# A tuned two-layer transformer kernel: the second bf16 part of q and k written by GpSimd's own subtraction instead of by a ScalarE copy

## The chip, the core and the metric

The kernel runs on one core of a Trainium2 chip. The metric is device time in microseconds, of which smaller is better. In the rows below PE is TensorE, DVE is VectorE, ACT is ScalarE, POOL is GpSimd and SP is SyncE, which here only issues DMAs.

## What is computed

The input x has 16 sequences ("batches" below) of 512 tokens and 128 features. Four blocks follow one another, each added to its own input: attention, a gated feed-forward network, a second attention with RMS-normed q and k, and a linear layer with a routed LoRA term.

```
x = x + _L0_attn_ref(_layernorm(x, axis=-1), ...)
x = x + _L0_ffn_ref(_layernorm(x, axis=-1), ...)
x = x + _L1_attn_ref(_layernorm(x, axis=-1), ...)
x = x + _L1_ffn_ref(_layernorm(x, axis=-1), ...)
```

Each attention has 16 heads of 8 features over 512 keys: `scores = softmax(q k^T * scale)`, then `scores @ v`, then a projection. The first attention is called layer 0 below, the second one layer 1.

## The kernel before

**Slots and units.** The 32 attentions (16 batches, two layers) run one after the other, each in a *slot* of 64 *units*. In a unit PE makes one tile of scores for the current attention (`attend_score`, L1203) and one tile of scores for the next one (`max_score`, L1193, 26 units ahead). ACT takes the exponential of the first (L719), and DVE takes the row maxima of the second (L932). Every fourth unit PE multiplies four tiles of exponentials with v (L1218). All other work is put between units by tables (`PE_AT`, `ACT_AT`, `DVE_AT`, `POOL_AT`, `SP_AT`), which give the unit at which an engine's in-order program comes to it. The tables fix the order on each engine, and semaphores fix the rest. From slot 2 to slot 27 layer 0 runs in even slots and layer 1 in odd ones.

**Three bf16 parts.** The score matmuls are bf16, so q and k (f32, tiles `qf` and `kf`, 128x512) are split into three bf16 parts in `qp` and `kp`: part 0 is q rounded, part 1 the rounded residual, part 2 the rounded residual of that. ACT writes `qf` (L748) and part 0 (`take_part0`, L697). POOL forms the residual in place (`residual1`, L585). ACT copies it to bf16 (`take_part1`, L697), and POOL subtracts again (`residual2`, L591).

**From parts to stacks.** When part 2 is there, SP writes the parts to DRAM with three DMAs (`parts_out`, L432: first q's, then k's). When they have landed it reads them back as stacked rows, in two halves of four DMAs each (`stack_half`, L446: `q_stack`, `k_stack`). The first `max_score` of the next attention, at unit 38 of the slot, needs the first half.

**What is near.** In an even slot (the group "M2" of the tables, for layer 1) the order on POOL is: residual of q1, a normalisation of `o_raw` (L597), part 2 of q1, residual of k1, part 2 of k1, then the residuals of the next batch's q0 and k0 (group "P0"), part 2 of k0, `norm_factors` for the third layer norm (L578 and L580), and part 2 of q0. On SP the third quarter of the row maxima (`max_rows`, L453) stands between `parts_out` of k1 and `stack_half`. On ACT `apply_norm` (L725) waits for `norm_factors`, and PE's transposes (L1156) wait for it.

Of the kernel before, what the change touches and what calls it, by code (L numbers as in the profile page):

```python
# [8 lines left out]
ALU = mybir.AluOpType  # L9
# [42 lines left out]
         "M2": {"qt": 16, "kt": 19, "v1": 19},  # L52
         "E": {"pr1": 22, "xt3": 40, "rt": 45, "ct": 65, "out": 68}}
ACT_AT = {"A": {"save0": 36, "save1": 67},
          "P0": {"part0_q0": 8, "part0_k0": 16, "part1_q0": 27, "part1_k0": 27},
          "P0_fast": {"part0_q0": 4, "part0_k0": 8, "part1_q0": 10, "part1_k0": 17},
          "S0": {"xn0a": 44, "xn0b": 58},
          "M1": {"xn1": 25, "xn2": 50, "sq0": 55, "sq1": 58},
          "M2": {"part0_q1": 17, "part0_k1": 21, "part1_q1": 19, "part1_k1": 22},
          "E": {"xn3a": 33, "xn3b": 38, "gexp": 50}}  # L60
DVE_AT = {"A": {"inv0": 43, "inv1": 73},
          "S0": {"st0a": 27, "st0b": 27, "mo0": 31, "fa0": 34},
# [45 lines left out]
def due_table(tables):  # L108

    due = {}  # L110
    for group, b, slot, shift in GROUPS:
        for table in tables:
            for name, at in table[group].items() if group in table else ():
                due.setdefault(name, {})[UNITS * slot + shift + at] = b
    return due


PE_DUE, ACT_DUE, DVE_DUE, POOL_DUE, SP_DUE = (due_table([t]) for t in (PE_AT, ACT_AT, DVE_AT, POOL_AT, SP_AT))
# [5 lines left out]
def at(due, name, t):  # L124

    return due[name][t] if name in due and t in due[name] else None
# [71 lines left out]
def build(nc, T, out_dram):  # L198
    ctx = ExitStack()
    with ctx:  # L200
# [48 lines left out]
        qf = [[sb(f"{c}f{l}", [128, SEQ]) for c in "qk"] for l in (0, 1)]  # L249
        qp = [[sb(f"{c}p{l}", [128, PARTS, SEQ], BF16) for c in "qk"] for l in (0, 1)]  # L250
# [80 lines left out]
        resid1 = [sem(f"{c}_resid1") for c in ("q0", "k0", "q1", "k1")]  # L331
        part0 = [sem(f"part0_{l}") for l in (0, 1)]

        part1 = [sem(f"{c}_part1") for c in ("q0", "k0", "q1", "k1")]
# [219 lines left out]
        def _(pool):  # L554
# [27 lines left out]
            def residual1(l, n, b):  # L582

                pool.wait_ge(part0[l], 2 * b + n + 1)
                pool.tensor_tensor(qf[l][n][:, :], qf[l][n][:, :], qp[l][n][:, 0, :], ALU.subtract  # L585
                                   ).then_inc(resid1[2 * l + n], 1)

            def residual2(l, n, b):

                pool.wait_ge(part1[2 * l + n], b + 1)  # L590
                pool.tensor_tensor(qp[l][n][:, 2, :], qf[l][n][:, :], qp[l][n][:, 1, :], ALU.subtract  # L591
                                   ).then_inc(part2[2 * l + n], 1)

# [56 lines left out]
            for t in TIMES:  # L650
                for n in (0, 1, 2):
                    b = at(POOL_DUE, f"nr{n}", t)
                    if b is not None:
                        newton_round(n, b)
                for n in (0, 1):
                    b = at(POOL_DUE, f"sc{n}", t)
# [5 lines left out]
                b = at(POOL_DUE, "nf1", t)  # L662
                if b is not None:
                    norm_factors(1, b)
                for c in range(NH):
                    b = at(POOL_DUE, f"um{c}", t)
                    if b is not None:
                        up_mul(c, b)
                for l in (1, 0):
                    for n in (0, 1):  # L670
                        b = at(POOL_DUE, f"r1_{'qk'[n]}{l}", t)
                        if b is not None:
                            residual1(l, n, b)
                        b = at(POOL_DUE, f"r2_{'qk'[n]}{l}", t)
                        if b is not None:
                            residual2(l, n, b)
                b = at(POOL_DUE, "nf3", t)
                if b is not None:
                    norm_factors(3, b)
                b = at(POOL_DUE, "mix", t)  # L680
                if b is not None:
                    mix(b)
                b = at(POOL_DUE, "nf0", t)
                if b is not None:
                    norm_factors(0, b)
                b = at(POOL_DUE, "nf2", t)
# [8 lines left out]
        def _(act):  # L695
            def copy(dst, src):
                return act.activation(dst, src, ACT.Copy)  # L697
# [54 lines left out]
                need(act, rows_out[l][n], 48 * b)  # L752
                copy(qp[l][n][:, 0, :], qf[l][n][:, :]).then_inc(part0[l], 1)

            def take_part1(l, n, b):
                act.wait_ge(resid1[2 * l + n], b + 1)
                copy(qp[l][n][:, 1, :], qf[l][n][:, :]).then_inc(part1[2 * l + n], 1)

            def take_max(l, quarter, b):
                act.wait_ge(written[f"m{l}"], 4 * b + quarter + 1)  # L760
                if quarter < 2:
# [39 lines left out]
            for n in (0, 1):  # L801
                if n == 0:
                    act.wait_ge(bq_ready, 1)
                take_qk(0, n, 0)
                take_part0(0, n, 0)
                take_part1(0, n, 0)
            weights_out()
            apply_norm(0, x_in, range(TT), 1)
            for t in TIMES:
# [11 lines left out]
                b = at(PE_DUE, "xt0", t)  # L821
                if b is not None:
                    take("xt0", xnt[0][:, :], b)
                for l in (0, 1):
                    for n in (0, 1):
                        b = at(PE_DUE, (("q0", "k0"), ("qt", "kt"))[l][n], t)
                        if b is not None:
                            take_qk(l, n, b)
                        b = at(ACT_DUE, f"part0_{'qk'[n]}{l}", t)
                        if b is not None:  # L830
                            take_part0(l, n, b)
                        b = at(ACT_DUE, f"part1_{'qk'[n]}{l}", t)
                        if b is not None:
                            take_part1(l, n, b)
                b = at(ACT_DUE, "xn3a", t)
                if b is not None:
                    apply_norm(3, x3, (0, 1), b)
                b = at(ACT_DUE, "xn3b", t)
                if b is not None:
                    apply_norm(3, x3, (2, 3), b)  # L840
                b = at(PE_DUE, "xt3", t)
                if b is not None:
                    take("xt3", xnt[3][:, :], b)
                b = at(ACT_DUE, "gexp", t)
                if b is not None:
                    gate_exp(b)
                b = at(PE_DUE, "ct", t)
                if b is not None:
                    take_coef(b)
                b = at(ACT_DUE, "xn0a", t)  # L850
                if b is not None:
                    apply_norm(0, x_in, (0, 1), b)
                b = at(ACT_DUE, "xn0b", t)
                if b is not None:
                    apply_norm(0, x_in, (2, 3), b)
                b = at(ACT_DUE, "xn1", t)
                if b is not None:
                    apply_norm(1, x1, range(TT), b)
                b = at(PE_DUE, "xt1", t)
                if b is not None:  # L860
                    take("xt1", xnt[1][:, :], b)
                for c in range(NH):
                    b = at(PE_DUE, f"g{c}", t)
                    if b is not None:
                        gate_tanh(c, b)
                    b = at(PE_DUE, f"u{c}", t)
                    if b is not None:
                        take_up(c, b)
                b = at(ACT_DUE, "xn2", t)
                if b is not None:  # L870
                    apply_norm(2, x2, range(TT), b)
                b = at(PE_DUE, "xt2", t)
                if b is not None:
                    take("xt2", xnt[2][:, :], b)
                for half in (0, 1):
                    b = at(ACT_DUE, f"sq{half}", t)
# [488 lines left out]
```

## Time and profile before

| | |
|---|---|
| median of 3 runs | 1851.92 us (1851.39 to 1855.57) |
| the profiled execution | 1849.55 us, of which the span is 1847.7 us |
| busy: PE, DVE | 1711.7 us (93%), 1560.2 us (84%) |
| busy: ACT, POOL | 1419.9 us (77%), 515.4 us (28%) |
| mean granted TensorE clock | 0.978 of full speed |

The busy times say how full an engine is over the whole span. Matmuls are pipelined, so that a busy PE is not PE at its peak. What limits a stretch is read from the chain of work that ended last and from what each idle time waited for. An even slot lasts some 48 us and an odd one some 61 us.

### The profile page before, as it was taken

The numbers are of one execution on the slowest core, as the hardware profiler recorded it, in microseconds if no ns is written. First come the engines' busy times: TensorE is split into PE (matmuls) and PEld (weight loads), VectorE is DVE, ScalarE is ACT, GpSimd is POOL, SyncE is SP. The second block draws the span as 40 slices with busy tenths as digits, with TensorE's granted clock in tenths as the row PEclk, the third lists the DMA queues.
The fourth block names the chain that finished last, engine by engine and source line by source line (L and its number), as shares of the span: only waits on it lengthen the run. The fifth ranks groups of instructions, "written<-read, shape, count | busy, mean of one in ns | idle before, by whom it ended". The sixth has DMA issues, their size and how long they took to land.

```text
span 1847.7 us, 32248 instructions
## 1 busy us (share of the span) xinstructions
PE 1711.7 (93%) x10958; PEld 654.7 (35%) x10958; DVE 1560.2 (84%) x3443; ACT 1419.9 (77%) x2921; POOL 515.4 (28%) x771
## 2 busy tenths in 40 slices
PE   4999899999999999999999999999999999999994
PEld 1233233434333343333334333343433334334333
DVE  3988789898998989898898898989899898888981
ACT  2788678787877978778787877878787787777872
POOL 3124132241222324122141313214122332422311
PEclk9999899999999999999999999999999999999996
DMA  5232324232142422315133151423315242132310
GB/s 126 65 82 73 96 49 127 49 85 80 43 134 48 116 61 65 100 38 139 47 85 90 38 128 37 128 48 81 84 43 133 48 111 59 36 66 77 85 35 24
DMA packets 162646, 141.35 MB, mean 76 GB/s; under 512 B 38762, under 2 KB 144051, under 8 KB 162483
## 3 DMA queue, kind: packets, MB, share of 16 engines
q1 hardware_dynamic: 160562, 138.18, 29.0%
q8 instruction: 88, 1.44, 0.4%
q10 hardware_dynamic: 1920, 1.11, 0.2%
q14 instruction: 76, 0.61, 0.1%
HBM read 77.38 MB, written 55.57 MB: 72 GB/s over the span
## 4 chain that ended last, share of the span: by engine, by line
PE 62%; DVE 12%; ACT 11%; DMA 6%; issue 4%; SPq 3%; POOL 2%; DVEq 0%; POOLq 0%; ACTq 0%
PE ps L1218 19%; PE ps L1203 15%; DVE neg_max L932 8%; PE ps L1193 7%; PE ps L1239 7%; ACT probs L719 6%; PE ps L1156 4%; DMA k_stack<-k_rows 3%; PE ps L1244 3%; PE ps L1232 3%; PE ps L1283 3%; ACT xn L725 2%; PE ps L1289 2%; DMA k_rows<-kp 2%; DVE bn L908 1%
## 5 line engine op out<-in xcount | busy, mean ns | idle before, releaser
L932 DVE TENSOR_REDUCE neg_max<-ps 128x1 f32<-128x512 f32 x2048 | 1305.9, 679 | 131.4 <-PE ps L1193 125.4
L719 ACT ACTIVATE probs<-ps 128x512 f32<-128x512 f32 x2048 | 1099.2, 594 | 272.9 <-PE ps L1203 271.2
L1193 PE MATMUL ps<-k_stack,q_stack 48*128 48x512 bf16 x2048 | 691.0, 391 | 57.9 <-DVE neg_max L932 38.0
L1203 PE MATMUL ps<-q_stack,k_stack 50*128 50x512 bf16 x2048 | 657.5, 387 | 24.1 <-ACT probs L719 14.3
L1218 PE MATMUL ps<-probs,v_aug 128*32 128x512 f32 x4096 | 555.3, 615 | 0.1
L1203 PEld LDWEIGHTS ps<-q_stack,k_stack 50*128 50x128 bf16 x2048 | 153.7, 94 | 593.3 <-ACT probs L719 355.4
L1193 PEld LDWEIGHTS ps<-k_stack,q_stack 48*128 48x128 bf16 x2048 | 162.1, 93 | 215.8 <-DVE neg_max L932 166.3
L578 POOL TENSOR_TENSOR rstd<-vpe,half_neg 128x4 f32<-128x4 f32 x64 | 64.6, 1010 | 268.6 <-DVE vpe L923 268.6
L597 POOL TENSOR_TENSOR o_raw<-o_raw,rden_all 128x512 f32<-128x512 f32 x64 | 81.6, 1276 | 177.9 <-DMA rden_all<-rden_rows 177.9
L1218 PEld LDWEIGHTS ps<-probs,v_aug 128*32 128x32 f32 x4096 | 80.9, 108 | 138.7 <-issue 76.8
L725 ACT ACTIVATE xn<-x,shift,rstd 128x128 f32<-128x128 f32 x192 | 80.7, 487 | 29.2 <-POOL shift L580 29.2
L635 POOL TENSOR_TENSOR coef<-gating,rm 128x64 f32<-128x64 bf16 x64 | 16.8, 294 | 284.4 <-DVE gating L1040 284.4
L585 POOL TENSOR_TENSOR qf<-qf,qp 128x512 f32<-128x512 f32 x32 | 37.2, 1161 | 205.2 <-ACT qp L697 205.2
L628 POOL TENSOR_TENSOR ht<-up,gs 128x512 f32<-128x512 f32 x48 | 61.2, 1276 | 98.2 <-ACT up L697 98.0
L607 POOL TENSOR_TENSOR nw_t<-nw_y 128x128 f32<-128x128 f32 x48 | 19.2, 401 | 214.9 <-DVE nw_y L1012 212.4
L1244 PE MATMUL ps<-wo,o_raw 128*128 128x128 f32 x512 | 67.3, 286 | 9.6 <-POOL o_raw L597 9.6
L1244 PEld LDWEIGHTS ps<-wo,o_raw 128*128 128x128 f32 x512 | 61.2, 196 | 26.6 <-issue 16.0
L1156 PE MATMUL ps<-ident,xn 128*128 128x128 f32 x256 | 46.4, 310 | 23.4 <-ACT xn L725 22.6
L970 DVE TENSOR_TENSOR x<-ps,x 128x512 f32<-128x512 f32 x32 | 22.1, 691 | 42.0 <-PE ps L1283 21.7
L970 DVE TENSOR_TENSOR x<-ps,res 128x512 f32<-128x512 f32 x32 | 21.9, 686 | 39.7 <-PE ps L1244 39.7
L1239 PE MATMUL ps<-xnt,w_up 128*128 128x256 f32 x192 | 54.2, 404 | 0.0
L1239 PE MATMUL ps<-xnt,w_gate 128*128 128x256 f32 x192 | 50.6, 386 | 1.3 <-DVE gs L982 0.6
(104 smaller groups left out, 1520.8 us busy)
## 6 DMA issues: line engine op xcount, KB each, us to landing
q_stack<-q_rows SPq DMA_DIRECT2D x128, 192.0 KB, 3.7
k_stack<-k_rows SPq DMA_DIRECT2D x128, 192.0 KB, 4.8
rden_all<-rden_rows SPq DMA_DIRECT2D x64, 256.0 KB
q_rows<-qp SPq DMA_DIRECT2D x32, 384.0 KB, 2.6
k_rows<-kp SPq DMA_DIRECT2D x32, 384.0 KB, 2.8
q_rows<-qp SPq DMA_DIRECT2D x32, 256.0 KB, 2.9
k_rows<-kp SPq DMA_DIRECT2D x32, 256.0 KB, 2.9
x_in<-in_L_attn_x SPq DMA_DIRECT2D x16, 256.0 KB, 3.3
```

The costliest lines, as they stand in the source:

```text
L578: pool.tensor_tensor(rstd[k][:, :], vpe[k][:, :], half_neg[:, :], ALU.pow).then_inc(rstd_ready[k], 1)
L597: pool.tensor_tensor(o_of(l, b)[:, c, :], o_of(l, b)[:, c, :], rden_all[:, c, :], ALU.mult).then_inc(att_ready[l], 1)
L628: pool.tensor_tensor(ht[:, c, :], up[:, :], gs[:, :], ALU.mult).then_inc(ht_done, 1)
L719: act.activation(probs[:, g % RING, :], home("score", (l, b, u)), ACT.Exp).then_inc(exps, 1)
L725: last = act.activation(xn[k][:, t, :], x[:, t, :], ACT.Identity, bias=shift[k][:, t:t + 1], scale=rstd[k][:, t:t + 1])
L932: dve.tensor_reduce(neg_max[l][:, pair // 2, col:col + 1], home("max", (l, b, n)), AX.X, ALU.max, negate=True).then_inc(max_taken, 1)
L1156: return pe.transpose(dst, src, ident[0:n, 0:n])
L1193: pe.matmul(home("max", (l, b, m)), q_stack[l][row:row + KROWS, pair, tok:tok + 128], k_stack[l][row:row + KROWS, pair, :], start=True, st ...
L1203: pe.matmul(home("score", (l, b, u)), k_stack[l][row:row + AROWS, pair, tok:tok + 128], q_stack[l][row:row + AROWS, pair, :], start=True, ...
L1218: last = pe.matmul(acc[32 * j:32 * j + 32, :], v_of(l, b)[:, kt, 8 * e + 2 * group + pp, :], probs[:, (g + j) % RING, :], start=(s == 0 an ...
L1239: return pe.matmul(dst[:, 256 * half:256 * half + 256], w, xt[:, 256 * half:256 * half + 256], start=True, stop=True)
L1244: last = pe.matmul(by_tile(dst)[:, t, :], o_of(l, b)[:, c, 128 * t:128 * t + 128], wo[l][:, c, :], start=c == 0, stop=c == 1)
```

## The change

ACT's copy `take_part1` goes, with its places in the table. POOL's `residual1` gets a second subtraction of the same operands ahead of the one that it had: it writes part 1 in bf16 straight away. The f32 residual is still formed, for part 2. `residual2` now waits for two semaphores, both of POOL itself. Its lines move by three and more (L591 becomes L594, L697 becomes L700, L719 becomes L722).

```diff
-          "P0": {"part0_q0": 8, "part0_k0": 16, "part1_q0": 27, "part1_k0": 27},
-          "P0_fast": {"part0_q0": 4, "part0_k0": 8, "part1_q0": 10, "part1_k0": 17},
+          "P0": {"part0_q0": 8, "part0_k0": 16},
+          "P0_fast": {"part0_q0": 4, "part0_k0": 8},
...
             def residual1(l, n, b):
 
                 pool.wait_ge(part0[l], 2 * b + n + 1)
+                pool.tensor_tensor(qp[l][n][:, 1, :], qf[l][n][:, :], qp[l][n][:, 0, :], ALU.subtract
+                                   ).then_inc(part1[2 * l + n], 1)
                 pool.tensor_tensor(qf[l][n][:, :], qf[l][n][:, :], qp[l][n][:, 0, :], ALU.subtract
                                    ).then_inc(resid1[2 * l + n], 1)
 
             def residual2(l, n, b):
 
                 pool.wait_ge(part1[2 * l + n], b + 1)
+                pool.wait_ge(resid1[2 * l + n], b + 1)
                 pool.tensor_tensor(qp[l][n][:, 2, :], qf[l][n][:, :], qp[l][n][:, 1, :], ALU.subtract
                                    ).then_inc(part2[2 * l + n], 1)
...
-            def take_part1(l, n, b):
-                act.wait_ge(resid1[2 * l + n], b + 1)
-                copy(qp[l][n][:, 1, :], qf[l][n][:, :]).then_inc(part1[2 * l + n], 1)
```

On POOL, in the middle of slot 2 (the first slot that has the order of all later even ones), stood before (a digit behind a name is the layer):

```order
L585 TENSOR_TENSOR qf1<-qf1,qp1 128x512 [waits part0_1]
L597 TENSOR_TENSOR o_raw01<-o_raw01,rden_all 128x512 [waits rden_in0]
L591 TENSOR_TENSOR qp1<-qf1,qp1 128x512 [waits q1_part1]
L585 TENSOR_TENSOR kf1<-kf1,kp1 128x512 [waits part0_1]
L591 TENSOR_TENSOR kp1<-kf1,kp1 128x512 [waits k1_part1]
L585 TENSOR_TENSOR qf0<-qf0,qp0 128x512 [waits part0_0]
L585 TENSOR_TENSOR kf0<-kf0,kp0 128x512 [waits part0_0]
L591 TENSOR_TENSOR kp0<-kf0,kp0 128x512 [waits k0_part1]
L591 TENSOR_TENSOR qp0<-qf0,qp0 128x512 [waits q0_part1]
```

And in the same place on POOL now:

```order
L585 TENSOR_TENSOR qp1<-qf1,qp1 128x512 [waits part0_1]
L587 TENSOR_TENSOR qf1<-qf1,qp1 128x512
L600 TENSOR_TENSOR o_raw01<-o_raw01,rden_all 128x512 [waits rden_in0]
L594 TENSOR_TENSOR qp1<-qf1,qp1 128x512 [waits q1_resid1,q1_part1]
L585 TENSOR_TENSOR kp1<-kf1,kp1 128x512 [waits part0_1]
L587 TENSOR_TENSOR kf1<-kf1,kp1 128x512
L594 TENSOR_TENSOR kp1<-kf1,kp1 128x512 [waits k1_resid1,k1_part1]
L585 TENSOR_TENSOR qp0<-qf0,qp0 128x512 [waits part0_0]
L587 TENSOR_TENSOR qf0<-qf0,qp0 128x512
L585 TENSOR_TENSOR kp0<-kf0,kp0 128x512 [waits part0_0]
L587 TENSOR_TENSOR kf0<-kf0,kp0 128x512
L594 TENSOR_TENSOR kp0<-kf0,kp0 128x512 [waits k0_resid1,k0_part1]
```

Two more instructions stand in front of part 2 of k1 (the first L594 that writes kp1), and four in front of part 2 of k0; no wait for ACT's copy is left between a residual and part 2. From slot 4 on `norm_factors` stands behind part 2 of k0.

On ACT in the same slot stood before:

```order
L748 ACTIVATE qf1<-ps,qn_scaled 128x512 [waits qt_written]
L719 ACTIVATE probs<-ps 128x512 [waits scores]
L697 ACTIVATE qp1<-qf1 128x512 [waits qrows_out1,qt_read]
L719 ACTIVATE probs<-ps 128x512 [waits pv,scores]
L697 ACTIVATE kp0<-kf0 128x512 [waits krows_out0,k0_read]
L719 ACTIVATE probs<-ps 128x512 [waits scores]
L697 ACTIVATE qp1<-qf1 128x512 [waits q1_resid1]
L748 ACTIVATE kf1<-ps,norm_w 128x512 [waits kt_written]
L719 ACTIVATE probs<-ps 128x512 [waits scores] x2
L697 ACTIVATE kp1<-kf1 128x512 [waits krows_out1,kt_read]
L719 ACTIVATE probs<-ps 128x512 [waits pv,scores]
L697 ACTIVATE kp1<-kf1 128x512 [waits k1_resid1]
```

And now:

```order
L751 ACTIVATE qf1<-ps,qn_scaled 128x512 [waits qt_written]
L722 ACTIVATE probs<-ps 128x512 [waits scores]
L700 ACTIVATE qp1<-qf1 128x512 [waits qrows_out1,qt_read]
L722 ACTIVATE probs<-ps 128x512 [waits pv,scores]
L700 ACTIVATE kp0<-kf0 128x512 [waits krows_out0,k0_read]
L722 ACTIVATE probs<-ps 128x512 [waits scores]
L751 ACTIVATE kf1<-ps,norm_w 128x512 [waits kt_written]
L722 ACTIVATE probs<-ps 128x512 [waits scores] x2
L700 ACTIVATE kp1<-kf1 128x512 [waits krows_out1,kt_read]
```

The two copies that waited for POOL's residual (q1_resid1 and k1_resid1) are gone. The orders of PE, DVE and SP are unchanged.

## Rows read from the trace of the kernel before

**Rows 1.** The page: the chain that ended last, shares by engine

```profile
PE 62%; DVE 12%; ACT 11%; DMA 6%; issue 4%; SPq 3%; POOL 2%; DVEq 0%; POOLq 0%; ACTq 0%
```

**Rows 2.** Groups by form: busy us, mean ns | idle before, releaser

```profile
L697 ACT ACTIVATE kp<-kf 128x512 bf16<-128x512 f32 x64 | 41.0, 641 | 12.9 <-POOL kf L585 12.9
...
L585 POOL TENSOR_TENSOR kf<-kf,kp 128x512 f32<-128x512 f32 x32 | 37.2, 1162 | 12.5 <-ACT kp L697 12.4
...
L591 POOL TENSOR_TENSOR kp<-kf,kp 128x512 bf16<-128x512 f32 x32 | 37.1, 1159 | 41.9 <-ACT kp L697 41.9
```

**Rows 3.** The chain in slot 10, in order of time: start us, us, what

```profile
616.58 0.52 ACT qp L697
...
619.24 1.17 POOL kf L585
...
620.44 0.64 ACT kp L697
...
621.14 1.17 POOL kp L591
...
623.24 2.56 DMA k_rows<-kp
...
627.19 5.49 DMA k_stack<-k_rows
```

**Rows 4.** The chain again, in slots 2 and 24

```profile
180.59 1.16 POOL kp L591
...
1389.38 1.17 POOL kp L591
```

**Rows 5.** Timeline of POOL in slot 10: start us, us, instruction [idle before <-releaser]

```profile
615.16 1.17 POOL L585 TENSOR_TENSOR qf<-qf,qp 128x512 f32<-128x512 f32 x1 [11.43 <-ACT qp L697]
616.28 1.28 POOL L597 TENSOR_TENSOR o_raw<-o_raw,rden_all 128x512 f32<-128x512 f32 x1
617.52 1.17 POOL L591 TENSOR_TENSOR qp<-qf,qp 128x512 bf16<-128x512 f32 x1
619.24 1.16 POOL L585 TENSOR_TENSOR kf<-kf,kp 128x512 f32<-128x512 f32 x1 [0.56 <-ACT kp L697]
621.14 1.16 POOL L591 TENSOR_TENSOR kp<-kf,kp 128x512 bf16<-128x512 f32 x1 [0.74 <-ACT kp L697]
622.26 1.16 POOL L585 TENSOR_TENSOR qf<-qf,qp 128x512 f32<-128x512 f32 x1
623.38 1.17 POOL L585 TENSOR_TENSOR kf<-kf,kp 128x512 f32<-128x512 f32 x1
626.04 1.15 POOL L591 TENSOR_TENSOR kp<-kf,kp 128x512 bf16<-128x512 f32 x1 [1.50 <-ACT kp L697]
627.37 1.01 POOL L578 TENSOR_TENSOR rstd<-vpe,half_neg 128x4 f32<-128x4 f32 x1 [0.17 <-DVE vpe L923]
628.46 0.20 POOL L580 TENSOR_TENSOR shift<-neg_mean,rstd 128x4 f32<-128x4 f32 x1
```

**Rows 6.** Timeline of SP's queue in slot 10

```profile
622.39 1.32 SPq L432 DMA_DIRECT2D k_rows<-kp  x3
624.00 1.30 SPq L453 DMA_DIRECT2D q_stack<-m_parts  x2
625.85 0.81 SPq L446 DMA_DIRECT2D q_stack<-q_rows  x2
```

**Rows 7.** Who waited for whom: us in total, times, longest us

```profile
PE ps L1193 <- DMA k_stack<-k_rows: 14.7, 13, 4.5
```

**Rows 8.** Timeline of PE, in slots 6 and 22

```profile
416.38 0.63 PE L1156 MATMUL ps<-ident,xn 128*128 128x128 f32 x4 [0.44 <-ACT xn L725]
...
1292.71 0.39 PE L1193 MATMUL ps<-k_stack,q_stack 48*128 48x512 bf16 x2 [1.86 <-DMA k_stack<-k_rows]
```

**Rows 9.** Timeline of ACT in slot 10

```profile
629.67 0.87 ACT L725 ACTIVATE xn<-x,shift,rstd 128x128 f32<-128x128 f32 x2
```

**Rows 10.** Timeline of DVE in slot 10

```profile
619.84 0.59 DVE L938 CAST neg_high<-neg_max 128x16 bf16<-128x16 f32 x1
```

More of the change, by code:

```diff
@@ L54 @@
 ACT_AT = {"A": {"save0": 36, "save1": 67},
-          "P0": {"part0_q0": 8, "part0_k0": 16, "part1_q0": 27, "part1_k0": 27},
-          "P0_fast": {"part0_q0": 4, "part0_k0": 8, "part1_q0": 10, "part1_k0": 17},
+          "P0": {"part0_q0": 8, "part0_k0": 16},
+          "P0_fast": {"part0_q0": 4, "part0_k0": 8},
           "S0": {"xn0a": 44, "xn0b": 58},
           "M1": {"xn1": 25, "xn2": 50, "sq0": 55, "sq1": 58},
-          "M2": {"part0_q1": 17, "part0_k1": 21, "part1_q1": 19, "part1_k1": 22},
+          "M2": {"part0_q1": 17, "part0_k1": 21},
           "E": {"xn3a": 33, "xn3b": 38, "gexp": 50}}
@@ L805, in _ @@
                 take_part0(0, n, 0)
-                take_part1(0, n, 0)
             weights_out()
@@ L831, in _ @@
                             take_part0(l, n, b)
-                        b = at(ACT_DUE, f"part1_{'qk'[n]}{l}", t)
-                        if b is not None:
-                            take_part1(l, n, b)
                 b = at(ACT_DUE, "xn3a", t)
```

## Prediction

> **What bounds the kernel now.** I first read the shares of the chain that ended last. PE has 62% of it, DVE 12%, ACT 11%, DMA 6% and POOL 2% [rows 1]. So this is a pipeline of units led by PE, and ACT, which the change relieves, is only a ninth of the chain. POOL, which the change loads, is idle most of the time, but it is on the chain all the same, and the question is where.
>
> The chain in order of time tells. In slot 10 it leaves the pipeline of units at ACT's copies, and goes through POOL's residual of k (619.24), ACT's copy of it to bf16 (620.44), POOL's part 2 of k (621.14), the DMA of the parts to DRAM (from 623.24, 2.56 us) and the DMA that reads the stack back (from 627.19, 5.49 us, so landed at 632.68) [rows 3]. PE's first `max_score` of layer 1 stood waiting for that. The chain takes this route in seven even slots, 2, 10, 12, 14, 18, 22 and 24; the first and the last of them are in [rows 4]. In the others PE mostly waits there too, but something else is as late. In all PE waited 14.7 us in 13 places for a stack [rows 7], up to 1.86 us in one slot [rows 8]; the longest wait, of 4.5 us, is the program's start. So the latency from "part 0 of q1 is there" to "the stack has landed" is what an even slot hangs on, and the change rebuilds its first links.
>
> **ACT: what is removed.** ACT loses 64 copies (16 batches, two layers, q and k). One takes 641 ns [rows 2], and keeps the next instruction off for 0.52 us (at 616.58 in [rows 3]), so 64 x 0.52 = 33 us in all. ACT also loses the waits for POOL's residual ahead of them, 12.9 us before the k copies [rows 2]. Of this only what lies on the chain can shorten anything. In an even slot that is the copy of q1 at 616.58. It delays kf1, thereby part 0 of k1, thereby POOL's residual of k1. But as shown next, POOL will not be free for that residual when it comes earlier. The other copies lie behind the start of the POOL work on which the stack hangs, or beside PE and DVE work. Nothing that they free lets PE pass unit 38 before the stack is there. I count ACT's gain as zero in the slots where the stack binds. Its cover is the stack wait, and were that gone, the gain would be up to the 0.52 us of one copy per slot.
>
> **POOL: what is added.** The new subtraction reads f32 and bf16 and writes bf16, as L591 does: 1159 ns [rows 2]. That is the same form, so I need no bound from elsewhere. Back to back such instructions start 1.12 us apart (622.26 to 623.38), `o_raw` takes 1.24 us of POOL, and an instruction that waits for the one before it starts 0.08 us after its end (627.37 + 1.01 = 628.38, then 628.46) [rows 5]. Now I lay out slot 10 anew, from the same start, since part 0 of q1 comes as before:
>
> - q1's part 1 at 615.16, q1's residual at 616.28, `o_raw` at 617.40, q1's part 2 at 618.64.
> - k1's part 1 at 619.76. Its input was ready at 619.24 already before the change [rows 5], so POOL itself is the limit. k1's residual at 620.88, and k1's part 2 at 620.88 + 1.16 + 0.08 = 622.12, done at 623.28.
> - Before, it was done at 621.14 + 1.16 = 622.30. So part 2 of k1 is 0.98 us late. The account is 2 x 1.12 added and 1.26 given back by the two waits for ACT that go (0.56 and 0.74 us) and by the smaller gap.
>
> The three DMAs of k follow at once (622.39 against an end at 622.30), the stack's DMAs follow their landing at 625.80 (623.24 + 2.56, then 625.85) [rows 3, 6], and nothing in between has slack: the maxima's rows at 624.00 to 625.30 also move back, to 624.7, and still end before the parts land at 626.8. So the stack lands 0.98 us late, at about 633.66, and PE stands there 0.98 us longer.
>
> - POOL goes on: q0's two at 623.24 and 624.36, k0's at 625.48 and 626.60, k0's part 2 at 627.84, L578 at 628.96, L580 from 630.05 to 630.25. Before, L580 ended at 628.66, and ACT came to its use only at 629.67 [rows 5, 9], with 1.0 us to spare. It is 1.6 us later now, so ACT stalls for 0.64 us (630.31 less 629.67), with exponentials queued behind it, and PE's transposes behind both. This runs beside the stack's wait; the larger of the two counts.
>
> **Sum.** In the seven slots in which the chain takes the POOL route nothing else is as late, and the whole 0.98 us passes: 6.9 us. In seven more (slots 4, 6, 8, 16, 20, 26 and 30, with the same POOL order or nearly) part of it replaces another wait. In slot 6 PE waited 0.44 us for ACT's xn right behind [rows 8], so that 0.54 us of the stack's lateness is left, while ACT's 0.64 us passes; I take 0.7 us each, 4.9 us. Slots 28 and 29 have their stacks far ahead of need, and the start is bound by SP's queue of weight loads; I count nothing there. Together 11.8 us. The profiled execution took 1849.55 us, 1847.7 us of span and 1.85 us around it, so it would take 1861.4 us. The median of the runs shown lies 2.4 us above that execution, so 1863.7 us against 1851.92, 0.6% slower.
>
> **DVE against POOL.** DVE's cast of 16 columns took 0.59 us in slot 10 and ended at 620.43 [rows 10], just behind the end of POOL's instruction at 620.40 [rows 5]: it waited for it. An instruction of that kind that meets a POOL instruction waits for its end, up to 1.16 us, and POOL will now be busy from 615.2 to 631 nearly without a gap.
>
> The Trainium skill (Advanced Engine Details and Errata, VectorE Performance Modes) says that VectorE's second SBUF port is shared with GpSimd, and that GpSimd instructions and two-port VectorE instructions block each other. The trace agrees, with this row. By the page's rule alone the move of work to GpSimd is bad wherever VectorE is near the bound, which is the second rival.
>
> **The rivals.**
>
> 1. *The forecast*, chance 0.62: late part 2, late stack, 1863.7 us. Its own range is 1858 to 1868.
> 2. *DVE is held up more than the stack*, chance 0.18. Two small DVE instructions per even slot meet POOL between units 22 and 31. One paid some 0.43 us until now, the other nothing. Average waits of half an instruction (0.58 us each) would add 0.73 us, which hides beside the 0.98 us of the stack. At the worst they add 2 x 1.16 - 0.43 = 1.9 us, some 1 us more than I counted, in 14 slots. I price it at half of that, 7 us more: 1871 us. For it speaks that the slots repeat exactly, so that an unlucky meeting repeats 13 times; against it that DVE has short idle times there.
> 3. *It comes out even*, chance 0.12. Only the seven chain slots pay (6.9 us), and in the seven others ACT's saved 0.52 us comes through in full: 6.9 - 3.6 = 3.3 us, or 1855 us. Against it speaks that POOL's order and start are the same in all of them.
> 4. *Faster*, chance 0.08. The ACT copies on the route are worth it and POOL's extra work isn't late: 0.52 + 0.64 + 0.07 us in seven slots, 8.6 us, or 1843 us. This needs part 2 of k1 no later than before, that is two added subtractions in the 1.26 us that POOL gets back, 0.63 us each instead of 1.12. The row of the same form [rows 2] speaks against it.
>
> That the change does nothing is excluded: the order shows 64 copies fewer on ACT and 64 subtractions more on POOL.
>
> **How the numbers follow.** A measurement of this kernel can tell about 0.3% (5.6 us) from no change. Slower by more: the first two cases and a little of the third, 0.83. Within 0.3%: most of the third, and what the first may lose, 0.10. Faster: 0.07. The range is 1856 to 1873: from the even case up to the DVE case, with the fourth left out below and the worst of the second above.
>
> **What would show it.** In the profile after, ACT's bf16 copies fall from 128 to 64 and its busy time by about 41 us; POOL's busy time rises by 64 x 1.16 = 74 us, to 590 us. From the start of q1's first subtraction to the end of k1's part 2 it takes 8.1 us instead of 7.1. PE's waits at the first `max_score` grow by 0.5 to 1 us in nearly each even slot, some 10 us in total, and ACT's xn waits for POOL's shift once per even slot, about 0.6 us. An even slot lasts some 49 us, an odd one as before. I am wrong if even slots keep their length of some 48 us, or if the stack's wait is the same as before; and if DVE's small instructions near unit 25 take 1 us and more, the second rival is at work.

## The result, and the profile after

Over 20 runs each, the changed kernel takes 1863.45 us (median; 1849.69 to 1874.08) and the kernel before 1852.33 us (1846.6 to 1870.22). The ratio is 1.0057, with a 95% interval of 1.0039 to 1.0075: slower by 0.6%, where 1863.7 us had been forecast. The profiled execution took 1862.63 us, with a span of 1860.8 us and a mean granted TensorE clock of 0.971.

The page of the changed kernel, its busy times and its chain:

```profile
PE 1716.2 (92%) x10958; PEld 653.0 (35%) x10958; DVE 1573.8 (85%) x3443; ACT 1391.2 (75%) x2857; POOL 585.4 (31%) x835
...
PE 60%; DVE 11%; ACT 8%; POOL 8%; DMA 6%; issue 4%; SPq 3%; POOLq 0%; DVEq 0%; ACTq 0%
```

POOL had 2% of the chain [rows 1] and now has 8%; ACT had 11% and has 8%. The work moved from one engine's share of the chain to another's.

The groups by form of the changed kernel, the new subtraction, the old one and what is left of the copies:

```profile
L585 POOL TENSOR_TENSOR kp<-kf,kp 128x512 bf16<-128x512 f32 x32 | 37.1, 1161 | 3.5 <-ACT kp L700 3.5
L587 POOL TENSOR_TENSOR kf<-kf,kp 128x512 f32<-128x512 f32 x32 | 37.2, 1163 | 0.0
L594 POOL TENSOR_TENSOR kp<-kf,kp 128x512 bf16<-128x512 f32 x32 | 37.1, 1158 | 4.3
L700 ACT ACTIVATE kp<-kf 128x512 bf16<-128x512 f32 x32 | 21.0, 655 | 0.0
```

The new subtraction costs 1161 ns, the same as its form cost before [rows 2]. POOL's wait ahead of part 2 of k fell from 41.9 us in all [rows 2] to 4.3.

The timeline of POOL in slot 10 of the changed kernel answers to [rows 5]:

```profile
620.08 1.16 POOL L585 TENSOR_TENSOR qp<-qf,qp 128x512 bf16<-128x512 f32 x1 [11.42 <-ACT qp L700]
621.21 1.16 POOL L587 TENSOR_TENSOR qf<-qf,qp 128x512 f32<-128x512 f32 x1
622.32 1.28 POOL L600 TENSOR_TENSOR o_raw<-o_raw,rden_all 128x512 f32<-128x512 f32 x1
623.56 1.15 POOL L594 TENSOR_TENSOR qp<-qf,qp 128x512 bf16<-128x512 f32 x1
624.68 1.15 POOL L585 TENSOR_TENSOR kp<-kf,kp 128x512 bf16<-128x512 f32 x1
625.79 1.16 POOL L587 TENSOR_TENSOR kf<-kf,kp 128x512 f32<-128x512 f32 x1
627.10 1.16 POOL L594 TENSOR_TENSOR kp<-kf,kp 128x512 bf16<-128x512 f32 x1
```

From the first row's start to the last row's end it is 8.18 us; before, 615.16 to 622.30, it was 7.14. All starts but the last lie where the prediction had laid them out (1.12, 2.24, 3.48, 4.60 and 5.72 us behind the first). The last, which waits for the row above it, starts 0.15 us after that row's end, not 0.08.

The chain of the changed kernel in slot 10 answers to [rows 3] (start, us, what):

```profile
627.10 1.17 POOL kp L594
...
629.18 2.54 DMA k_rows<-kp
...
633.12 5.63 DMA k_stack<-k_rows
638.75 0.05 issue
638.80 0.39 PE ps L1188 x2
```

The DMAs take nearly what they took: the read-back was 5.49 us and is 5.63. PE's `max_score` starts 18.72 us after q1's first subtraction; before it was 17.56 (615.16 by [rows 5], to 632.72, 0.04 us behind the landing in [rows 3]). In slots 4, 6, 16 and 20 of this execution the chain takes another way. In slot 16:

```profile
960.55 1.16 POOL kp L594
961.71 0.97 POOL rstd L578
...
962.75 0.21 POOL shift L580
...
963.39 0.48 ACT xn L728
```

That is POOL's work for the next batch, then `norm_factors`, then ACT's normalisation, the second lateness in the prediction's sum. The waits of the changed kernel (total, times, longest):

```profile
ACT xn L728 <- POOL shift L580: 33.0, 30, 16.8
...
PE ps L1188 <- DMA k_stack<-k_rows: 17.6, 13, 4.6
...
PE ps L1151 <- DVE x L965: 5.2, 12, 0.4
```

PE's wait for a stack was 14.7 us [rows 7]. The last row is new: in each even slot from 4 to 26 PE now waits 0.42 or 0.43 us for DVE's `x`, some 9 us ahead of the first `max_score`. The kernel before has no such wait. The second rival comes back to it.

**Slots.** The windows of PE in three even slots of the changed kernel (16, 18, 22), each from its first `attend_score` to the next slot's; after the busy time come the granted clock, the DMA share and GB/s:

```profile
934.96:983.83 48.87, 46.48 (x316) 1.00 0.41 117
1043.77:1094.42 50.65, 46.42 (x317) 1.00 0.40 113
1263.18:1316.59 53.41, 49.35 (x316) 0.94 0.38 106
```

The same windows of the kernel before, slots 16 and 18 (all engines):

```profile
932.41:980.62 48.21, 46.34 (x316) 16.18 (x312) 44.44 (x94) 42.97 (x89) 14.13 (x20) 1.00 0.43 118
1042.02:1090.24 48.22, 46.31 (x316) 16.02 (x312) 44.54 (x94) 42.97 (x89) 14.13 (x20) 1.00 0.43 118
```

Slot 16 is 0.66 us longer. In slot 22 there is more: PE waited 2.17 us for the stack, and then ran at half clock. The timeline of PE there:

```profile
1292.47 0.60 PE L1188 MATMUL ps<-k_stack,q_stack 48*128 48x512 bf16 x2
1292.69 0.79 PE L1198 MATMUL ps<-q_stack,k_stack 50*128 50x512 bf16 x2
1295.65 0.39 PE L1188 MATMUL ps<-k_stack,q_stack 48*128 48x512 bf16 x2 [2.17 <-DMA k_stack<-k_rows]
...
1297.51 0.61 PE L1198 MATMUL ps<-q_stack,k_stack 50*128 50x512 bf16 x1
...
1300.36 0.63 PE L1188 MATMUL ps<-k_stack,q_stack 48*128 48x512 bf16 x1
```

A single score matmul takes 0.39 us at full clock and 0.60 to 0.63 us after 1296.8. The windows from 1294 to 1306 say the same (the granted clock, ahead of the DMA share, is 0.85, 0.50 and 0.80; 0.50 is 1.2 GHz of 2.4):

```profile
1294.00:1298.00 4.00, 2.35 (x13) 0.85 1.14 202
1298.00:1302.00 4.00, 4.00 (x21) 0.50 0.09 15
1302.00:1306.00 4.00, 4.00 (x29) 0.80 0.82 288
```

To read all executions alike I use one table. It is worked out from the windows of slots 4 to 27 of each profiled execution: twelve even slots, parted into those at full clock throughout and those with a stretch at half clock, and twelve odd slots. "Late by" is that of slot 10. The last column is the ratio of the runs to those of the kernel before on the same chip; one of e10's seven runs, at 1890.42 us, is slow and left out of it. All other columns show one execution each, and not a typical one everywhere: those of e5, e7 and e11 were the fastest of their runs (e7's 1852.64 us against a median of 1873.32), and e3's was the slowest (1898.10 against 1885.19).

| kernel | part 2 of k1 late by | even, full clock: mean us (slots) | even, part at half clock | odd, sum us | ratio |
|---|---|---|---|---|---|
| before | 0 | 48.45 (12) | none | 733.2 | |
| changed | 1.03 | 49.19 (10) | 54.4 (2) | 722.8 | 1.0057 |
| e11, changed again | 1.02 | 49.19 (11) | 56.0 (1) | 720.6 | 1.0060 |
| e12, layer 0 late | 1.02 | 49.10 (10) | 54.6 (2) | 724.1 | 1.0081 |
| e7, the same | 1.02 | 48.95 (10) | 52.0 (2) | 722.5 | 1.0125 |
| e2, layer 1 only | 1.01 | 48.92 (9) | 54.7 (3) | 729.7 | 1.0065 |
| e9, k1 only | 0.52 | 48.77 (10) | 51.6 (2) | 733.2 | 1.0051 |
| e10, q1 only | 0.52 | 48.67 (9) | 57.1 (3) | 731.7 | 1.0070 |
| e3, added work | 1.62 | 49.85 (9) | 54.3 (3) | 733.2 | 1.0190 |
| e1, layer 0 only | 0 | 48.49 (11) | 50.9 (1) | 729.7 | 1.0006 |
| e5, no copies | -1.19 | 48.19 (12) | none | 734.4 | 1.0008 |
| e8, k1 first | -0.80 | 48.56 (9) | 53.7 (3) | 726.8 | 1.0081 |

### The profile page after: what moved, and what is told of

Read it like the earlier page. It is cut to its first block, busy times and chain, and to the rows that moved or that the text cites. A ratio compares the mean times of both kernels' runs of the same rounds, so it can differ in the third digit from the quotient of the medians.

```text
span 1860.8 us, 32312 instructions
## 1 busy us (share of the span) xinstructions
PE 1716.2 (92%) x10958; PEld 653.0 (35%) x10958; DVE 1573.8 (85%) x3443; ACT 1391.2 (75%) x2857; POOL 585.4 (31%) x835
## 3 DMA queue, kind: packets, MB, share of 16 engines
q1 hardware_dynamic: 160562, 138.18, 28.7%
## 4 chain that ended last, share of the span: by engine, by line
PE 60%; DVE 11%; ACT 8%; POOL 8%; DMA 6%; issue 4%; SPq 3%; POOLq 0%; DVEq 0%; ACTq 0%
PE ps L1213 19%; PE ps L1198 15%; PE ps L1188 7%; PE ps L1234 7%; DVE neg_max L927 7%; ACT probs L722 4%; PE ps L1151 4%; DMA k_stack<-k_rows 3%; PE ps L1227 3%; PE ps L1278 2%; PE ps L1239 2%; ACT xn L728 2%; DMA k_rows<-kp 2%; PE ps L1284 2%; POOL qp L585 1%
## 5 line engine op out<-in xcount | busy, mean ns | idle before, releaser
L722 ACT ACTIVATE probs<-ps 128x512 f32<-128x512 f32 x2048 | 1098.8, 595 | 321.5 <-PE ps L1198 319.1
L585 POOL TENSOR_TENSOR qp<-qf,qp 128x512 bf16<-128x512 f32 x32 | 37.1, 1160 | 205.3 <-ACT qp L700 205.3
L965 DVE TENSOR_TENSOR x<-ps,x 128x512 f32<-128x512 f32 x32 | 22.1, 692 | 41.9 <-PE ps L1278 21.5
```

What stands on the lines that cost most here:

```text
L722: act.activation(probs[:, g % RING, :], home("score", (l, b, u)), ACT.Exp).then_inc(exps, 1)
```

## Experiments

The theory is that of the forecast: part 2 of k1 late, so the stack late, so PE late. Its rivals are that DVE, held up by POOL, carries the loss, and that the loss is somewhere else in the moved work (layer 0's part, the shift that ACT waits for).

### The two halves: layer 0 only, layer 1 only

Both start from the kernel before; e1 has the new form in layer 0 alone, e2 in layer 1 alone.

```diff
                 pool.wait_ge(part0[l], 2 * b + n + 1)
+                if l == 0:      # e2: l == 1
+                    pool.tensor_tensor(qp[l][n][:, 1, :], qf[l][n][:, :], qp[l][n][:, 0, :], ALU.subtract
+                                       ).then_inc(part1[2 * l + n], 1)
...
                 pool.wait_ge(part1[2 * l + n], b + 1)
+                if l == 0:
+                    pool.wait_ge(resid1[2 * l + n], b + 1)
```

> The change for layer 0 alone: ACT loses 32 of the 64 copies, layer 1 stays as before. Theory (late stack): part 2 of k1 and the stack keep their times, norm_factors is some 0.6 us later with 1.0 us to spare, so 0.997 to 1.001 of before. Rival (ACT's relief is worth something): two copies a slot fewer on ACT behind unit 27, 1 us x 14, 0.993. Rival (DVE held up by POOL's longer stretch, or any POOL work costs): half of the change's loss, 1.003.

> The change for layer 1 alone: POOL has two more subtractions ahead of part 2 of k1, layer 0 stays as before. Theory (late stack): the whole loss of the change, 1.005 to 1.006, and k1's part 2 ends 8.1 us after the start of q1's first subtraction as in the changed kernel. Rival (POOL's load as such, or the late norm_factors behind layer 0's subtractions): half or less of it, 1.003.

Measured: e1 1852.3 us, ratio 1.0006 (0.9987 to 1.0025); e2 1867.52 us, ratio 1.0065 (1.0034 to 1.0095). The whole loss comes with layer 1's part. In e1 part 2 of k1 ends 7.14 us after q1's first subtraction, as before, and even slots keep their length. In e2 it is 8.15 us, and all even slots from 4 to 26 have the stack on the chain. Layer 0's four subtractions per even slot cost nothing by themselves: 1.0 us of spare stood before ACT's use of the shift [rows 5, 9], and they alone don't use it up.

### More work in the same place

e3 is the kernel before, copies and all, with two more POOL subtractions of unused data ahead of k1's residual. No other line changes.

```diff
+            def pad(b):
+
+                pool.wait_ge(padded, 2 + 2 * b)
+                for k in (0, 1):
+                    pool.tensor_tensor(pad_out[k][:, :], pad_in[:, :], pad_part[:, :], ALU.subtract).then_inc(padded, 1)
+
             def residual1(l, n, b):

+                if l == 1 and n == 1:
+                    pad(b)
```

> The kernel before with two more POOL subtractions (128x512, on tiles of their own, results unused) ahead of k1's residual; ACT keeps all its copies. By the rows of before k1's part 2 is then 1.6 us late (2 x 1.12 less the 0.56 us that POOL idled there). Theory: this passes through the stack in 14 even slots less what other waits had covered, 14 x 1.4 = 20 us, 1.010 to 1.012, about twice the loss of the change. Rival (a late stack is absorbed, the change's loss came from elsewhere): under 1.004.

Measured: 1885.19 us, ratio 1.0190 (1.0158 to 1.0221), well above what was expected. Part 2 of k1 is 1.62 us late, and an even slot at full clock takes 49.85 us. Windows of slots 16 and 26, PE alone:

```profile
948.71:998.19 49.48, 46.43 (x317) 1.00 0.41 115
1503.39:1560.07 56.68, 51.92 (x318) 0.88 0.36 101
```

Slot 16 is 1.27 us longer than before. But this isn't a clean dose of a late part 2. ACT still copies k1's residual, and its queue is in order, so it now stands longer for POOL, and the exponentials behind it come late. Who waited for whom in e3:

```profile
ACT kp L711 <- POOL kf L597: 39.5, 17, 3.5
```

Before it was 12.9 us [rows 2]. PE's waits for exponentials grew from 14.3 us to 33.7. In slot 16 of e3 PE begins the `attend_score` of unit 36 at 29.94 us after the slot's start (28.69 before), so the whole lateness is there before the first `max_score` asks for the stack, and in slots 8 and 20, as long as slot 16, the chain doesn't pass the stack at all. So e3 shows that more POOL work in this place costs more, by the stack or by ACT; it doesn't show what a late part 2 costs alone.

Slot 26 is 7.2 us longer still, at a lower clock. Fourteen slots with 1.3 us are 18 us of the 32 by which the medians differ. The rest isn't placed in a typical run. In the profiled one, the slowest, slots 26, 28, 29 and 30 are 25 us longer than before, with the clock at 0.5 for 55 us in them.

### The stack taken out of the way

The first `max_score` of the next attention comes at unit 38 since `AHEAD` is 26. With 24 it comes two units later. e4 is the changed kernel with it, e6 the kernel before.

```diff
-AHEAD = 26
+AHEAD = 24
```

> The changed kernel with the max scores 24 units ahead instead of 26, so that the first one that needs a stack stands at unit 40 instead of 38, some 1.5 us later in an even slot. Theory: the stack's 0.98 us of lateness is covered, PE's waits for a stack mostly go, and the time is at or below that of before, 0.990 to 1.000. The row maxima come two units later, which has its own cost in no more than a few slots. Rival (loss by DVE or ACT, not by the stack): still 1.004 to 1.008.

> The kernel before with the max scores 24 units ahead instead of 26, the twin of the changed kernel with 24, which took 1.0473 of before with no wait of PE for a stack left in the even slots. Theory (late stack): with the stack's wait gone the two kernels differ by 0.002 or less, so 1.045 to 1.050. Rival (the change costs by DVE or ACT as well): this one is faster than its twin by 0.005, 1.042.

Measured: e4 1941.33 us, ratio 1.0473 (1.0447 to 1.0498); e6 1942.15 us, ratio 1.0494 (1.0464 to 1.0524). Fewer units ahead cost 4.7% of their own, so this is no way to a faster kernel, and I had not expected that in e4. But the pair tells what it was made for. PE's waits for a stack, in e4 and then in e6:

```profile
PE ps L1188 <- DMA k_stack<-k_rows: 4.6, 1, 4.6
```

```profile
PE ps L1193 <- DMA k_stack<-k_rows: 6.4, 2, 4.7
```

One wait is left in e4, at the start. With the stack early enough, the change has no loss: e4 stands 0.2% below e6, within the intervals (each against the kernel before on its own chip). At full clock its even slots are shorter than e6's, 50.57 us against 51.12.

The pair doesn't clear DVE, though. With 24 the even slots of both kernels hang on DVE: in slot 16 PE waits 1.77 us (e6) and 1.74 us (e4) for a small subtraction on the row maxima, which meets POOL in both, takes 1.05 and 1.01 us where it takes 0.16 alone, and is on the chain. And other DVE instructions meet POOL than at 26. DVE's busy time is 1572.0 us in e4 and 1581.4 in e6, so it falls with the change, where it rises by 13.6 us at 26 units ahead. The pair takes away the stack's wait and DVE's additional meetings together.

### No copies, and no work for POOL instead

e5 is the kernel before without the 64 copies; part 1 of q and k stays zero, and `residual2` waits for the residual. It leaves part 1 out of the computation and keeps every size and DMA.

```diff
-                pool.wait_ge(part1[2 * l + n], b + 1)
+                pool.wait_ge(resid1[2 * l + n], b + 1)
...
-                take_part1(0, n, 0)
```

> The kernel before without any of the 64 copies of part 1 and without anything in their place (part 1 stays zero, so the output lacks that part): ACT is relieved as by the change, POOL does no more than before, and its part 2 follows the residual at once. By the rows of before k1's part 2 ends some 1.2 us earlier than before. Theory: the stack comes earlier by that until the next wait binds (the third quarter's rows of maxima stand in SP's queue from 624.0 on, so 0.5 to 0.6 us of it count), an even slot gets 0.3 to 0.6 us shorter, 0.995 to 0.998. If ACT's copies had been a cost of their own, beyond the stack: 0.990 or less.

Measured: 1850.91 us, ratio 1.0008 (0.9983 to 1.0033), no gain, where 0.995 to 0.998 had been expected. Part 2 of k1 ends 1.19 us earlier, and the read-back starts 0.49 us earlier, as laid out. All even slots from 4 to 24 take 48.11 or 48.12 us. Before, the quiet ones took 48.22 or 48.23, and slots 10, 12, 22 and 24, in which the chain passed the stack, 48.33, 48.29, 49.43 and 48.62. Slot 16, PE alone:

```profile
925.34:973.46 48.12, 45.98 (x318) 1.00 0.43 118
```

So 48.12 us is what an even slot takes when the stack is early: the other chain of the slot, of row maxima, exponentials, `xn` and transposes, is 0.1 us below a quiet slot of before. The stack was a bound before, but with a second one directly below it. That is why lateness costs and earliness gives next to nothing: the twelve even slots together are 3.2 us shorter, less than the medians can tell. Of the 0.1 us not all belongs to the stack. In e1, where part 2 comes as before and layer 0's copies are gone, quiet slots take 48.14.

### Layer 0's POOL work later

In slots 4, 6, 16 and 20 the changed kernel's chain went through POOL's shift. e7 puts layer 0's subtractions behind `norm_factors`; e12 is the same kernel, run later beside the changed kernel (e11).

```diff
-           "P0": {"r1_q0": 31, "r1_k0": 31, "r2_q0": 40, "r2_k0": 38},
+           "P0": {"r1_q0": 40, "r1_k0": 40, "r2_q0": 41, "r2_k0": 41},
```

> The changed kernel with POOL's work on layer 0's parts put behind norm_factors (units 40 and 41 instead of 31 to 40). k1's part 2 is as late as in the changed kernel, but norm_factors no longer is, and DVE's small instruction of it meets POOL less. Theory: the layer 1 part of the loss stays and the layer 0 part goes, even slots 48.5 to 48.6 us instead of 48.9, 1.003 to 1.006. If the late norm_factors were the main cost: 1.000.

> The changed kernel itself once more, so that the two halves of its layer-1 part and the late order of layer 0 stand beside it on one chip: 1.0057 (1.004 to 1.0075), undisturbed even slots 48.87 us.

> The changed kernel with layer 0's subtractions behind norm_factors, on the same chip as the changed kernel. In the first run of it the slots that had been set by POOL's shift were shorter than with the change (slot 20: 48.54 instead of 48.88 us), yet its ratio to the kernel before was 1.0125 on another chip than the changed kernel's 1.0057. If that was the chip, this comes out 0.1 to 0.3% below the changed kernel beside it; if the late order itself costs, it is 0.5% and more above it.

Measured: e7 1873.32 us, ratio 1.0125 (1.0096 to 1.0155). On another chip e11 takes 1863.75 us, 1.0060 (1.0032 to 1.0087), and e12 1868.85 us, 1.0081 (1.0048 to 1.0113). The route through the shift is gone: slot 16 of e11, then of e12:

```profile
927.04:975.88 48.84, 46.50 (x318) 1.00 0.41 116
```

```profile
929.22:977.74 48.52, 45.95 (x316) 1.00 0.43 118
```

In e12 and e2 slot 16 takes 48.52 us, and in both the stack is on its chain; with the shift late too it is 48.84 (48.87 in the first execution of the change). So the second lateness was real, and binds in slots in which the stack comes early. Taking it away brings nothing over all runs: e12 is no faster than e11, rather 0.2% slower, which the intervals don't tell from nothing. e7's 1.0125 lies outside both, and why isn't settled. What is on record is the clock: the profiled execution of e7, at 1852.64 us, had 0.983, and its seven other runs, of 1862.98 to 1877.43 us, had 0.961 to 0.970.

### k first

e8 was meant to beat both kernels: the new form in layer 0 only and late (with part 0 of k0 at unit 24 instead of 16), and in layer 1 the order changed so that ACT makes k1's part 0 before q1's part 1, and POOL forms k1's residual before q1's part 2.

```diff
-          "M2": {"part0_q1": 17, "part0_k1": 21, "part1_q1": 19, "part1_k1": 22},
+          "M2": {"part0_q1": 17, "part0_k1": 20, "part1_q1": 21, "part1_k1": 22},
...
-           "M2": {"sc0": 5, "sc1": 9, "r1_q1": 10, "r2_q1": 19, "r1_k1": 19, "r2_k1": 22},
+           "M2": {"sc0": 5, "sc1": 9, "r1_q1": 10, "r1_k1": 18, "r2_q1": 19, "r2_k1": 22},
```

> A version meant to beat both: layer 0's part 1 by POOL as in the change, behind norm_factors; layer 1's by ACT as before, but ACT makes part 0 of k1 before part 1 of q1, layer 0's part 0 of k comes later (unit 24), and POOL does k1's residual before q1's part 2. By the rows of before k1's part 2 then ends some 1.3 us earlier, of which SP's queue lets 0.5 to 0.9 us through. Theory: even slots 47.6 to 47.9 us instead of 48.2, and fewer long waits of PE, 0.994 to 0.998. Rival (latency of the parts is no longer what binds): 1.000.

Measured: 1865.58 us, ratio 1.0081 (1.0053 to 1.0110), where 0.994 to 0.998 had been expected. Part 2 of k1 is ready 0.8 us earlier, but q's part 2 is later, and its three DMAs stand directly ahead of k's. SP's queue in slot 10 of e8:

```profile
621.74 1.57 SPq L432 DMA_DIRECT2D q_rows<-qp  x3
623.42 1.99 SPq L432 DMA_DIRECT2D k_rows<-kp  x3
```

k's DMAs take 1.99 us to issue instead of 1.32 [rows 6], and the parts are in DRAM 23.86 us after the start of a quiet slot (23.44 before). In slots 10, 18 and 22 the stack came still later and the clock fell.

### Half of the lateness

e9 has the new form for k1 alone and e10 for q1 alone, both on the kernel before.

```diff
+                if l == 1 and n == 1:      # e10: n == 0
+                    pool.tensor_tensor(qp[l][n][:, 1, :], qf[l][n][:, :], qp[l][n][:, 0, :], ALU.subtract
+                                       ).then_inc(part1[2 * l + n], 1)
```

> The kernel before with the new form for k1 alone: one more subtraction in front of part 2 of k1, and one wait for ScalarE fewer. Laid out from the rows of slot 10: part 1 of k1 at 619.24, its residual 1.12 us later, part 2 1.30 us after that, at 621.66 instead of 621.14, so 0.52 us late: from q1's first subtraction to the end of part 2 it takes 7.65 us (7.14 before, 8.17 with the whole change). If the loss follows the lateness in proportion, undisturbed even slots take 48.5 us and the ratio is 1.003 (1.002 to 1.004). If lateness is first taken up by slack and costs more the larger it is, because the clock falls behind long waits, they take 48.2 to 48.4 us and the ratio is 1.000 to 1.002.

> The kernel before with the new form for q1 alone: one more subtraction ahead of o_raw, and ScalarE without the copy of q1 that stood ahead of kf1. POOL comes to the residual of k1 0.52 us later (619.76 instead of 619.24), ScalarE's copy of it is still waited for, and part 2 of k1 is 0.52 us late: 7.66 us. If only the lateness of part 2 counts, the time equals that of the new form for k1 alone within 0.1%. If the copy of q1 that ScalarE no longer makes is worth something on the way to kf1, this one is the faster of the two by up to 0.5 us in 14 slots, 0.4%.

Measured: e9 1867.82 us, ratio 1.0051 (1.0021 to 1.0080); e10 1872.53 us, ratio 1.0070 (1.0033 to 1.0107). The lateness is 0.52 us in both, as laid out. Slot 16 behaves as expected, with 48.36 and 48.38 us, 0.15 us more than before.

e9 is the cleanest dose here. PE has no wait for DVE's `x` in it, and in slot 16 it begins unit 36 at 28.70 us after the slot's start (28.69 before), so what the slots pay comes behind the stack. Quiet slots 8 and 20 pay nothing (48.23 us), slot 16 pays 0.15 and slot 10 pays 0.92. So a late stack by itself costs.

But the medians lose as much as with the whole change. The twelve runs of e9 lie in two groups, five from 1847.6 to 1859.4 us with mean clocks of 0.975 to 0.983, and seven from 1867.1 to 1872.2 with 0.962 to 0.970. Slots 16 and 18 of e10:

```profile
928.09:976.47 48.38, 46.35 (x316) 1.00 0.43 119
1039.39:1096.57 57.18, 53.28 (x316) 0.85 0.36 100
```

In slots 18, 22 and 26 PE waited 2.5 to 2.6 us for the stack and ran at half clock from then on for 17.1 us, and the slots took 7.7 to 9.0 us longer than before. The kernel before had a wait of 1.86 us at most in slots 4 to 26 [rows 8], and none of them had the clock down in its profiled execution. Both expectations for the size were wrong: it neither follows the lateness in proportion nor stays under it.

## Why the prediction was right, point by point

- **Where the bound is.** Right for the slots on the stack's chain. Layer 1's part carries the loss (e2), layer 0's none (e1), a late stack costs with PE in time up to it (e9), and the chain of the changed kernel passes there in slots 8 to 14, 18 and 22 to 26. That the whole 0.6% of the medians is this isn't shown, since half the lateness costs as much (e9, e10).
- **POOL laid out anew: part 2 of k1 late by 0.98 us.** Measured 1.03. The term was off by the gap before a dependent subtraction, 0.15 us instead of 0.08.
- **The whole 0.98 us passes in seven slots, 0.7 us in seven more.** Right in the sum, rough in the parts. The ten even slots from 4 to 26 that kept full clock are 8.2 us longer in sum than the same ten before, 0.82 us each; over 14 slots that would be 11.4 us where 11.8 were forecast. But 2.4 us of it are slot 18 alone. Of the chain's slots, 10, 12, 14 and 24 pay 1.16, 0.58, 0.74 and 0.36 us, not 0.98. Slots 4, 16 and 20, in which the stack comes early, pay 0.66 us, not through the stack but through POOL's shift, which the sum had at 0.64. With the shift in time (e2, e12) slot 16 pays 0.3. There the stack lands 0.66 us later than before in e2 and 0.84 in e12, not 1.03, since its read-back was shorter (4.46 and 4.66 us for the last DMA of the half, 4.79 before). And before, PE had waited 0.44 us for `xn` behind it in this slot, which covers part of that, as the prediction had said for slot 6.
- **The clock, which the sum had at nothing.** The first size that failed, though the total hides it. Of the 13.1 us between the two profiled spans the twelve even slots make 19.4, of which slots 6 and 22, with half clock, make 11.2; odd slots give back 10.4; the first four slots give back 0.8; and from slot 28 on 5.0 are lost, 4.2 of them in slot 30, where the clock fell for 6.8 us behind a wait of 2.23 us. The forecast had 11.8 us from 14 even slots and nothing elsewhere.
- **ACT's gain counted as zero.** Right: with the copies gone and POOL spared, 0.1 us per quiet slot (e5). The prediction's gain of up to 0.52 us per slot, were the stack's wait gone, fits e4's 0.55 us, but DVE's meetings with POOL differ there too. ACT's busy time fell by 28.7 us, not 41: its instructions overlap, and each copy had held up the next by 0.52 us at most, as [rows 3] had said.
- **PE's waits for the stack grow by some 10 us, and xn's by 0.6 us a slot.** Wrong as signs to look for: they grew by 2.9 us each, xn's in 12 more places. PE, ACT and DVE come later to the wait themselves, so the wait stays short while the slot gets longer: in slot 16 PE begins unit 36 at 29.30 us after the slot's start, 0.61 us later than before, and the slot is 0.66 us longer. The length of the slot was the sign that held.
- **Odd slots as before.** Wrong, and not settled. Their sum fell by 10.4 us in this execution and by 12.6 in e11, since fewer of them had a stretch at half clock (6.8 us of it in all against 30.6). What PE did before such a stretch doesn't tell the two apart: in every odd slot from 5 to 27 of both kernels PE waits 1.22 us for a row maximum, 36 us after the slot's start, and within 2.3 us of that wait's end the clock falls in eight of twelve slots before, and in two of twelve with the change. Slot 9 of the kernel before, then of the changed kernel:

```profile
540.95:602.36 61.41, 58.95 (x377) 0.97 0.21 49
```

```profile
547.15:607.28 60.13, 57.50 (x377) 1.00 0.23 50
```

  In even slots the clock takes as much back, in slots 6 and 22 (55.46 and 53.42 us against 48.23 and 49.43). Only the kernels with the new form in both layers show the short odd slots fully (720.6 to 724.1 us). Over 32 runs the changed kernel's mean granted clock is 0.972, and over 60 runs of the kernel before it is 0.973. So the two effects nearly cancel in this kernel, and the difference of the medians is about what slots at full clock pay. That the forecast met the median to 0.2 us is luck on top of a sound sum: e7 and e12, with the same lateness, lose 0.8 to 1.25%. The half doses lack most of the gain in odd slots, and lose 0.5 to 0.7% where the lateness of their slots at full clock gives 0.2%. Why odd slots keep their clock with the new form in both layers, no run here tells.
- **Rival 2, DVE.** Its mechanism is there, and mis-sized: DVE's busy time grew by 13.6 us, 1 us a slot, where the average case had been put at 0.73. In slot 16 three small instructions meet POOL, not two. DVE's cast, and POOL's instruction that it met:

```profile
952.44 1.11 DVE L933 CAST neg_high<-neg_max 128x16 bf16<-128x16 f32 x1
```

```profile
952.35 1.17 POOL L585 TENSOR_TENSOR kp<-kf,kp 128x512 bf16<-128x512 f32 x1
```

  The cast, 0.17 us where it meets nothing, ends at 953.55 with POOL's at 953.52. Before, it took 0.60 us in this slot. It and the small subtraction behind it (0.61 us, 0.16 before) make DVE's `x` 0.51 us late, and PE waits 0.43 us for it. So DVE's lateness does reach PE, in the changed kernel, e11, e2, e7 and e12. The chain of slots 10 and 16 doesn't pass there, since the stack and the shift come later still. And e9 and e10 lose 0.5 to 0.7% without this wait. No run at 26 units ahead has these meetings without a late part 2, so what they would cost alone is open.
- **Rivals 3 and 4.** The new form costs the full 1.16 us, and the start of the route doesn't move; neither case came about.

The Trainium skill (SBUF — State Buffer, SBUF: two separate sides) calls the port pair that VectorE and GpSimd share an exclusive lock, held for the whole instruction, with the loser blocked. The cast above agrees: it ends 0.03 us behind POOL's instruction. In its Summary: rules for kernel authors the page advises to schedule whichever of the two is off the critical path. In the changed kernel the blocked engine is off the chain: the blocking makes PE wait 0.43 us per even slot, beside later waits that hide it. In e4 and e6 a blocked subtraction is on the chain.

## What to carry to other kernels

Work taken off a relieved engine is worth what the path through it is worth, and a path that two things bind equally pays for lateness and gives nothing for earliness; test that with a kernel in which the work is simply absent (e5) before moving it. Lay out the receiving engine's in-order queue instruction by instruction: that gave the lateness to 0.05 us. Work put in to make a delay (e3) delays everyone who waits for that engine, so look who else waits before reading it as a dose. Where TensorE has waits of 1.2 us and more, a small delay wasn't paid in proportion here, so measure the clock of the slots behind the wait, and many runs.

## What the hardware showed that was not expected

- **The clock falls behind some short waits of PE and not behind others of the same length.** Behind the wait of 1.22 us in odd slots it fell in eight of twelve before, and in two of twelve after. In slot 6 of the changed kernel a wait of 1.55 us (it ends 0.05 us after the stack's landing, though the profile puts it down to an exponential) is followed by 13.7 us at 1.2 GHz, in slot 22 one of 2.17 us by 6.8 us; slot 18 waited 2.35 us and kept its clock. In slots 18, 22 and 26 of e10 it had fallen some 0.5 us before the wait of 2.5 to 2.6 us ended. In slot 6's stretch a transpose group takes 1.1 us instead of 0.63 [rows 8].
- **The landing of the same DMAs varies with the slot, and mostly repeats in it.** k's parts land 24.5 us after the start of slots 8, 10, 14, 16 and 20 of the changed kernel, and 26.3 and 26.4 us in slots 18 and 22; there the long waits are, in e10, e8 and e12 too.
- **POOL starts the next instruction before the profile ends the last.** Starts are 1.12 us apart with durations of 1.16 us; only a dependent one waits for the end, and 0.15 us more.
